# DLRM tower on one core: fifteen tables looked up in place of twelve, and gathers that wait for lookups in place of memsets

## What is computed

```python
e = jnp.stack([tbl_0[ids[:, 0]], ..., tbl_25[ids[:, 25]]], axis=1)
combined = jnp.concatenate([dense_features[:, None, :], e], axis=1)      # 512 x 27 x 128
interactions = jnp.einsum('bnd,bmd->bnm', combined, combined)
z = jnp.concatenate([dense_features, interactions[:, _TRIU_I, _TRIU_J]], axis=1)
h = jnp.concatenate([z, r_dense_features], axis=1)
h = jnp.maximum(h @ W_top1 + b_top1, 0.0)      # 607 -> 512
h = jnp.maximum(h @ W_top2 + b_top2, 0.0)      # 512 -> 256
y = h @ W_top3                                 # 256 -> 1
```

## Time and profile before

| | us |
|---|---|
| median of 3 runs | 147.07 |
| lowest, highest | 146.13, 147.31 |
| the profiled execution | 146.84 |
| its span | 145.0 |

### The profile page before, as it was taken

How to read it: one execution, slowest core, us unless ns; L and a number is a source line. 1 busy time by engine, 2 the same in 40 slices (tenths; PEclk the granted TensorE clock), 3 DMA queues, 4 the chain that set the end, 5 groups by cost and what they waited for, 6 DMA issues and landing times.

```text
span 145.0 us, 3567 instructions
## 1 busy us (share of the span) xinstructions
PE 112.2 (77%) x1525; PEld 90.7 (63%) x1525; DVE 62.1 (43%) x124; ACT 50.5 (35%) x104; POOL 82.3 (57%) x120
## 2 busy tenths in 40 slices
PE   6988899999994699744223533289999999899993
PEld 2464578888882688622211311289999899689791
DVE  2999999999999945000000000041015015005010
ACT  4659829497775624100000000104104203500432
POOL 1999998999999899898989898900000000000000
PEclk9999999999999999975555555559999999999999
DMA  4899999598789221111211111100000000000000
GB/s 136 281 253 268 269 244 277 124 262 197 226 276 347 80 58 37 42 49 46 49 49 42 52 38 52 38 23 0 5 5 5 0 5 5 0 5 5 5 0 1
DMA packets 5535, 13.96 MB, mean 96 GB/s; under 512 B 1712, under 2 KB 2100, under 8 KB 5392
## 3 DMA queue, kind: packets, MB, share of 16 engines
q1 hardware_dynamic: 3558, 9.88, 23.9%
q0 software_dynamic: 1792, 3.67, 10.2%
q10 hardware_dynamic: 170, 0.18, 0.5%
HBM read 13.73 MB, written 0.00 MB: 95 GB/s over the span
## 4 chain that ended last, share of the span: by engine, by line
PE 45%; POOL 24%; issue 19%; DMA 6%; ACT 5%; ACTq 0%
POOL rows_sb L332 18%; PE ps_gram L398 17%; PE ps_a L363 9%; PE ps_a L436 9%; POOL unread L340 7%; PE ps_h L452 4%; DMA rows_sb<-tbl,ids_sb 4%; PE ps_rows L377 2%; ACT xt L644 2%; DMA ids_sb<-ids 2%; ACT table_sb L682 1%; PE ps_h L466 1%; PE ps_a L425 1%; PE ps_h L479 1%; PE ps_rows L466 1%
## 5 line engine op out<-in xcount | busy, mean ns | idle before, releaser
L332 POOL DMA_INDIRECT rows_sb<-tbl,ids_sb x56 | 60.6, 1083 | 11.4 <-issue 8.9
L363 PE MATMUL ps_a<-onehot,part_sb 125*128 125x512 f32 (+2 forms) x212 | 50.8, 390 | 2.1 <-DVE part_sb L561 1.3
L363 PEld LDWEIGHTS ps_a<-onehot,part_sb 125*128 125x128 f32 x212 | 38.1, 192 | 11.3 <-DVE part_sb L561 3.2
L398 PE MATMUL ps_gram<-xt 128*27 128x27 f32 x1024 | 25.3, 230 | 23.5 <-issue 22.7
L398 PEld LDWEIGHTS ps_gram<-xt 128*27 128x27 f32 x1024 | 20.1, 148 | 27.8 <-issue 25.9
L552 DVE TENSOR_SCALAR onehot<-idrow,row_id 125x1024 fp32r<-125x1024 int16 (+1 forms) x51 | 36.1, 763 | 1.7 <-DMA idrow<-ids_by_table 1.6
L580 DVE STREAM_TRANSPOSE table_sb<-ps_gram 128x864 f32<-128x864 f32 x3 | 3.2, 1083 | 42.2 <-PE ps_gram L398 42.2
L340 POOL MEMSET unread<- 128x256 f32 x56 | 21.2, 379 | 0.0
L644 ACT COPY xt<-ps_rows 128x256 f32<-128x256 f32 (+2 forms) x32 | 9.2, 359 | 30.8 <-remote 30.8
L561 DVE TENSOR_TENSOR part_sb<-table_sb,part_sb 125x512 fp32r<-125x512 f32 (+1 forms) x24 | 16.0, 689 | 2.7 <-issue 2.7
L637 ACT COPY xt<-ps_a 128x512 f32<-128x512 f32 (+2 forms) x13 | 7.2, 556 | 25.4 <-PE ps_a L363 24.3
(11 more groups left out here) (36 smaller groups left out, 42.5 us busy)
## 6 DMA issues: line engine op xcount, KB each, us to landing
table_sb<-tbl SPq DMA_DIRECT2D x11, 448.0 KB
idrow<-ids_by_table SPq DMA_DIRECT2D x5, 256.0 KB
w_sb<-w SPq DMA_DIRECT2D x1, 1280.0 KB, 8.4
rows_sb<-tbl,ids_sb POOLq DMA_INDIRECT x56
table_sb<-tbl SPq DMA_DIRECT2D x1, 560.0 KB
table_sb<-tbl SPq DMA_DIRECT2D x10, 52.0 KB
w_sb<-w SPq DMA_DIRECT2D x1, 512.0 KB
dense_sb<-dense_by_column SPq DMA_DIRECT2D x1, 256.0 KB
```

Source lines behind the costliest of these rows:

```text
L332: pool.indirect_dma_start(rows_sb[:, t % ROWS_RING, GATHERED.index(f), :], None, tables[f], bass.IndirectOffsetOnAxis(ids_sb[:, t, f:f + 1 ...
L363: last = pe.matmul(ps_a[:, (h + piece) % 2, a:b], parts_sb[part][:, w, c * D:(c + 1) * D], unit_onehot(u, c)[:, member, a:b], start=(part ...
L398: last = pe.matmul(ps_gram[j * NPAD:j * NPAD + N, half, s * N:(s + 1) * N], x, x, start=True, stop=True)
```

## The change

Three tables of 1250 rows (1, 5 and 7) move from the gathers to the lookups: 15 lookups, four of them of 10 chunks, each of these in a unit of its own, and 11 gathered tables, so 44 gathers in 12 groups (4, 4, 3 for each tile). The order by hand is written anew: groups 0 to 5 behind lookups 3 to 8, 6 to 9 behind lookups 10 to 13, group 10 in the gram of tile 0, group 11 behind layer 2 of tile 0, none elsewhere. The memsets and their waits are gone. Six gathers are issued at once; before every third one after them GpSimd waits for one more lookup on TensorE's semaphore `lookup_done`. The wait of tiles 2 and 3 for the ring of `rows_sb` stays.

```diff
--- before.py
+++ after.py
@@ -47,15 +47,15 @@
 
 
 
-ONEHOT_TABLES = [4, 10, 11, 17, 19, 20, 24, 25, 3, 0, 8, 14]
+ONEHOT_TABLES = [4, 10, 11, 0, 17, 19, 1, 20, 24, 5, 25, 3, 7, 8, 14]
 VP = 125
-CHUNKS = [8] * 9 + [10] + [8] * 2
+CHUNKS = [8] * 3 + ([10] + [8] * 2) * 4
 CH = max(CHUNKS)
 SIZES = sorted(set(CHUNKS))
 FIRST_COLUMN = {c: sum(x + 1 for x in SIZES if x < c) for c in SIZES}
 ROW_COLUMNS = sum(c + 1 for c in SIZES)
 
-UNITS = [[0], [1, 2], [3, 4], [5, 6], [7, 8], [9], [10, 11]]
+UNITS = [[0], [1, 2], [3], [4, 5], [6], [7, 8], [9], [10, 11], [12], [13, 14]]
 UNIT_OF = [u for u, members in enumerate(UNITS) for _ in members]
 COMPARED = [CHUNKS[members[0]] - 1 for members in UNITS]
 BEFORE_UNIT = [sum(COMPARED[:u]) for u in range(len(UNITS))]
@@ -87,18 +87,18 @@
 
 GATHERED = [f for f in range(F) if f not in ONEHOT_TABLES]
 SOURCES = [f + 1 for f in GATHERED]
-GROUP_SIZES = [4, 4, 3, 3]
+GROUP_SIZES = [4, 4, 3]
 GROUP_STARTS = [sum(GROUP_SIZES[:i]) for i in range(len(GROUP_SIZES))]
 GROUPS = [(t, SOURCES[i:i + k]) for t in range(TILES) for i, k in zip(GROUP_STARTS, GROUP_SIZES)]
 assert sum(GROUP_SIZES) == len(SOURCES)
 
 
 
-AFTER_LOOKUP = [[], [], [], [0], [1], [2], [3], [4], [5], [6], [7], []]
-IN_GRAM = [8]
-IN_GAP = [9]
-BEFORE_GRAM = [[], [], [14, 15]]
-AFTER_LAYER2 = [[10, 11], [12, 13], []]
+AFTER_LOOKUP = [[], [], [], [0], [1], [2], [3], [4], [5], [], [6], [7], [8], [9], []]
+IN_GRAM = [10]
+IN_GAP = []
+BEFORE_GRAM = [[], [], []]
+AFTER_LAYER2 = [[11], [], []]
 ORDER = sum(AFTER_LOOKUP, []) + IN_GRAM + IN_GAP
 for _t in range(TILES - 1):
     ORDER += BEFORE_GRAM[_t] + AFTER_LAYER2[_t]
@@ -106,6 +106,8 @@
 GROUPS_UP_TO = [sum(t <= tile for t, _ in GROUPS) for tile in range(TILES)]
 
 WARM_UP = 13
+GATHERS_PER_LOOKUP = 3
+GATHERS_AHEAD = 6
 HIGH, LOW = PARTS = range(2)
 
 
@@ -274,9 +276,6 @@
             rows = tables[ONEHOT_TABLES[0]].rearrange("(p c) d -> p (c d)", c=CHUNKS[0])
             queue.dma_start(table_sb[a:b, 0, 0:n], rows[a:b, :]).then_inc(table_landed[0], 16)
 
-        unread = sb("unread", [P, 256], F32)
-        unread_written = sem("unread_written")
-
         block = ctx.enter_context(nc.Block())
 
         @block.sync
@@ -323,21 +322,19 @@
                 pool.iota(row_id[:, first + c:first + c + 1], [[1, 1]], base=1 - c, channel_multiplier=-c,
                           allow_small_or_imprecise_dtypes=True).then_inc(row_id_ready, 1)
             pool.wait_ge(ids_landed, 16)
-            paced = 0
+            issued = 0
             for g, (t, features) in enumerate(GROUPS):
                 if t >= ROWS_RING and t != GROUPS[g - 1][0]:
                     pool.wait_ge(group_turned, GROUPS_UP_TO[t - ROWS_RING])
                 for n in features:
                     f = n - 1
+                    if issued >= GATHERS_AHEAD and (issued - GATHERS_AHEAD) % GATHERS_PER_LOOKUP == 0:
+                        pool.wait_ge(lookup_done, (issued - GATHERS_AHEAD) // GATHERS_PER_LOOKUP + 1)
+                    issued += 1
                     pool.indirect_dma_start(
                         rows_sb[:, t % ROWS_RING, GATHERED.index(f), :], None, tables[f],
                         bass.IndirectOffsetOnAxis(ids_sb[:, t, f:f + 1], 0),
                     ).then_inc(group_landed[g], 16)
-
-                    if paced:
-                        pool.wait_ge(unread_written, paced)
-                    paced += 1
-                    pool.memset(unread[:, :], 0.0).then_inc(unread_written, 1)
 
         @block.tensor
         def _(pe):
```

## The result

The changed kernel took 124.83 us (median of 4, 123.11 to 125.7) beside 146.89 of the kernel before: a ratio of 0.843 (95% interval 0.833 to 0.853). The ratio goes by the two faster of the four runs (124.44 and 123.11), because the other two (125.22 and 125.7) were over 1.5% above the fastest. Forecast were 122.0 and a range of 118.8 to 129. The profiled execution took 124.44, its span 122.6. On this chip the prediction holds. The experiments then met two other chips on which the kernel before takes 117 us.

The account below looks back on a forecast made before the run. VectorE was full in the lookups and TensorE stalled in tile 0's gram; TensorE was to bound afterwards. Dense matmuls 22.0 us earlier plus 3.1 in the tail, 25.1 less: 121.7 profiled, median 122.0 us, range 118.8 to 129.

Parts of the forecast that it names:

- The gram: Tile 0's gram on TensorE: two halves of 2.00 us and group 10 between, 4.4 us in place of 36.3.
- Three more lookups: TensorE's lookups from lookup 3 to the last one's first piece: 49.9 us plus 1.0 for waits, ending at 70.
- VectorE: Compares in the lookups: without memsets VectorE ends at 63, TensorE bounds; at the old pace the first piece ends at 75.
- rival 1: Gathers hold up VectorE as memsets did: first piece ends at 75 to 76, total 127 to 128.5 us; 16%.
- The pacing: GpSimd's waits on lookups cost nothing; three gathers take 3.4 to 4.8 us against 4.2 for a mean lookup.
- Rival 4: The pacing doesn't clear the gram: two or three gathers fall into it, about 1.4 us each, total 125 us; 6%.
- Rival 2: Closer gathers starve TensorE in the lookups: some 52 matmuls come late by 12 us, total 134 us; 9%.
- The tail: Fewer turned groups: 0.45 us off after tile 0's layer 2, 1.0 after tile 1, 1.6 before tile 3's gram; together 3.1.
- Rival 3: The first gram's stall isn't GpSimd's and stays, with three lookups on top: 154 us, slower; 5%.

Follow-up runs that it names:

- experiment 3: Kernel before without its memsets and their waits, still 56 gathers and 12 lookups: 147.18 us, ratio 1.0035 to the kernel before.
- experiment 4: Changed kernel plus work beside tile 0's gram; twelve unread gathers: 140.53 us on chip R, 123.73 on Q; plain transfers or memsets on Q: 122.58 to 123.64.
- experiment 6: Changed kernel with the last group's three gathers waiting for tile 0's gram instead of the 13th lookup: 122.67 us, ratio 0.8385 to the kernel before.

## Why the prediction was right, and where it wasn't

By its own steps, on the chips on which it was made:

- *The gram.* "With GpSimd quiet" it was to take 4.4 us; it took 5.1 (70.75 to 75.86), 0.45 of them one "issue" pause at 74.22. That gathers are enough to hold TensorE up, without memsets (experiment 3) and not by the clock (experiment 4, chip R), is shown; whether memsets alone would do it on a crawling chip is not.
- *Three more lookups.* First piece to end at 70: 69.23. The sum of TensorE's lookups (four of 10 chunks, seven of 8) stood: with 1.0 for waits it was 50.9 us, and it took 51.0, from 18.25 (22.89 less the 4.64 of lookup 3) to 69.23. The 0.8 us lie ahead of it, where lookup 3 began 2.75 us sooner than 21.0, not 1.9.
- *VectorE.* Both cases were right in what they were for. Without memsets compares cost 0.66 and 0.40 from start to start and TensorE bounds, so VectorE, waiting for it now and then, has its last low half done at 65.98 and not at 63; at the pace of before the piece was to end at 75, and with memsets it ended at 75.78. The evidence taken against rival 1, one whole compare of 0.74 inside a gather, was the right row. The Trainium skill's exclusive lock (SBUF — State Buffer, "SBUF: two separate sides") is borne out for the memset, not for VectorE beside a gather. The other way round it may be: gathers took up to 1.99 us beside VectorE's work, though 1.02 beside many compares of 1024 columns, and 0.94 to 0.95 alone.
- *The pacing.* "I cost these waits at nothing" was right. The reason given was half right: GpSimd doesn't keep up with the lookups, it lags behind all waits. The gap between two gathers was taken as 0.17 us from rows in which a memset stood between them; it is 0.30, and a gather is 1.20 on average, so three take 4.5 us, more than the 4.2 of a mean lookup.
- *Rival 4* (a few gathers reach the gram) was therefore partly true: the last ones ended right ahead of it, and they cost 1.1 us of the 1.52 before the gram, by experiment 6, as a late copy.
- *Rival 2* (closer gathers starve TensorE in the lookups) was given 9%, for the reason that lookups had run beside gathers all along. It stayed away in the changed kernel, but experiment 3 has a stall in its lookups with gathers as close, 12.8 us by one late copy. What kept it away isn't known, so in this the forecast had luck.
- *The tail.* Forecast were 3.1 us less, and from the dense matmuls to the end of the span it went from 44.4 to 42.8, 1.6 less. The three places gave 0.3, 0.8 and 1.6, near what was worked out (0.45, 1.0, 1.6). Against them, the step from tile 0's dense matmuls to its layer 2, which holds tile 1's gram, took 0.5 us more than before, and tile 3's two gram halves 0.7 more. Pauses put down to "issue" are a part of it: 0.48 before 87.85 and 0.32 before 106.34. No work of GpSimd stands beside them. What they are wasn't tried.

The profiled execution was forecast at 121.7 and took 124.44. Of the 2.7 us, 0.35 lie before the gram, 0.7 in it, 0.1 behind it, 1.5 in the tail.

What the prediction did not see is that the crawl, its largest term (32 us), isn't a property of the kernel alone. Rival 3 had the difference right for the wrong reason: it priced a stall that stays at 154, 7 us above the kernel before. Where the crawl isn't there to be removed, the same terms remain, three more lookups and fewer turned groups, some +10 and -3 us, and 117 becomes about 123. The trace of before couldn't tell this; it showed the crawl beside gathers, with a releaser that no row names. A stall put down to "issue" deserved a doubt whether it comes on every chip. That the changed kernel was first measured on a chip that crawls, as the kernel before had been, was luck.

## What to carry to other kernels

Before paying instructions for the removal of a stall that the profile puts down to "issue", measure the kernel on another chip: here the change gains 22 us on one kind of chip and, by its variants, costs about 6 on the other. Keep GpSimd's gathers out of TensorE's closest sequences by their number and their place (the last ones behind the gram gave 1.7 us more); a wait does nothing on a queue that is already late. And don't expect memsets on GpSimd to be free while VectorE compares: they cost the changed kernel 6.65 us. To take them out of the kernel before gained nothing, because closer gathers stalled it elsewhere.

## What the runs showed of the hardware

- The same program behaves in one of two ways, and which one goes with the chip as far as one series on each can tell. On R TensorE's matmuls beside gathers drop to 5.7 per us (86 in 15 us), on Q the same program has 29 (434 in 15 us), with the same gathers of 0.94 us and 49 and 57 GB/s. By the time of the kernel before, P and the chip of the first runs are like R (146 to 147 us), S is like Q (117).
- On the crawling chips some signals are late as well, or what waits for them is: ScalarE's copy started 12.8 us after its lookup in experiment 3 (27.9 to 40.69), and 1.16 us after it in the changed kernel. On chip R, in the changed kernel, a copy started 2.7 us after its lookup (63.52 to 66.25), with VectorE's low halves and the last lookup behind it. In the six traces of Q and S the copy of the first piece starts 0.03 to 0.04 us after it. What makes matmuls and copies wait no row tells, and no run here takes gathers apart from their transfers on a crawling chip.
- A memset of 128 x 256 on GpSimd lengthens compares of VectorE (on average by 0.11 us over all compares, 0.38 for one that meets it); a gather doesn't (0.754 and 0.482 us on average beside gathers). Gathers take 0.95 us with VectorE idle (68.36) and as much as 1.99 beside its work (6.41, both in the changed kernel's trace); that VectorE is the cause was not tried.
